# The stores of the results move from SyncE's turn to the end of ScalarE's turn

## The reference

```python
W = weights[condition]                       # 16 matrices of 128 x 128
x = x + einsum('bct,bcd->bdt', x, W)         # the "rows", one per batch entry

mask = (arange(L) < length[:, None])
u_m = x * mask[:, None, :]
K = 2.0 * einsum('hn,hnl->hl', Cs, exp(P)).real     # one kernel per channel, 2048 taps
y = irfft(rfft(u_m, 2*L) * rfft(K, 2*L), 2*L)[..., :L]
y = (y + u_m * D[:, None]) * mask[:, None, :]
x = x + y
```

## Time and profile before

| | us |
|---|---|
| median of 3 runs | 2345.85 (2344.41 to 2353.0) |
| the profiled execution's own time | 2358.94 |
| its span, first to last instruction | 2357.1 |

### The profile page before, as it was taken

The page is one execution under the profiler, slowest core; times in us unless marked ns, Lnnn a source line. Parts: engine busy times, 40 slices in busy tenths (PEclk is TensorE's granted clock), DMA queues, the critical chain, the costliest instruction groups (busy, mean ns, idle before and its releaser), DMA issues.

```text
span 2357.1 us, 61717 instructions
## 1 busy us (share of the span) xinstructions
PE 2174.2 (92%) x15101; PEld 1880.7 (80%) x15101; DVE 1699.5 (72%) x3359; ACT 1505.9 (64%) x4354; POOL 1175.0 (50%) x1862
## 2 busy tenths in 40 slices
PE   6777778999999999999999999899999999999999
PEld 2222226888888888888888888799999999999998
DVE  4999204777777777777777777677777777777776
ACT  4556556777777777777777777455555555555555
POOL 0994503666666666666666666333333333333331
PEclk9999999999999999999999999999999999999999
DMA  8999999999999999999999999889989999899887
GB/s 319 420 414 369 394 359 330 316 315 315 314 316 318 317 317 318 320 315 317 320 319 311 323 316 307 241 251 262 268 253 267 266 270 259 259 261 264 254 260 223
DMA packets 337444, 716.26 MB, mean 304 GB/s; under 512 B 39554, under 2 KB 170884, under 8 KB 337412
## 3 DMA queue, kind: packets, MB, share of 16 engines
q1 hardware_dynamic: 300548, 581.66, 79.7%
q10 hardware_dynamic: 36864, 134.23, 14.0%
HBM read 395.92 MB, written 319.82 MB: 304 GB/s over the span
## 4 chain that ended last, share of the span: by engine, by line
PE 36%; DMA 28%; DVE 9%; SPq 8%; issue 8%; ACT 6%; ACTq 4%; DVEq 0%; POOL 0%
DMA decay<-x_scratch 12%; DMA toep<-k_scratch 11%; PE bank L900 7%; PE bank L902 6%; PE bank L901 6%; DMA row_x<-in_x 5%; PE bank L882 4%; DVE decay L803 4%; PE bank L945 4%; PE bank L869 3%; PE bank L937 3%; SPq L339 3%; SPq L355 2%; DVE e_lo L786 2%; ACTq L521 2%
## 5 line engine op out<-in xcount | busy, mean ns | idle before, releaser
L791 DVE TENSOR_TENSOR u_lo<-bank,u_hi 128x512 fp32r<-128x512 f32 x512 | 352.2, 688 | 252.7 <-ACT u_hi L603 246.7
L797 DVE TENSOR_TENSOR s_lo<-state,s_hi 128x128 fp32r<-128x128 f32 x768 | 291.8, 380 | 236.7 <-ACT s_hi L615 235.4
L900 PE MATMUL bank<-t_hi,u_hi 128*128 128x256 f32 x1024 | 361.7, 353 | 43.1 <-DMA toep<-k_scratch 42.5
L612 ACT ACTIVATE state<-bank 128x128 f32<-128x128 f32 x768 | 213.9, 279 | 286.8 <-PE bank L902 149.5
L803 DVE COPY_PREDICATED decay<-mask,bank 128x512 f32<-128x512 uint8 x512 | 379.1, 741 | 23.8 <-PE bank L902 3.6
L945 PE MATMUL bank<-toep,u_odd 128*128 128x128 f32 x2048 | 392.8, 273 | 0.0
L546 ACT ACTIVATE row_y<-bank 128x512 f32<-128x512 f32 x512 | 301.4, 589 | 138.2 <-ACT row_y L546 38.7
L489 POOL TENSOR_TENSOR x_lo<-row_x,x_hi 128x256 fp32r<-128x256 f32 x496 | 371.5, 778 | 0.0
L869 PE MATMUL bank<-row_x,w_sel 128*128 128x512 f32 x528 | 265.5, 630 | 94.2 <-DMA row_x<-in_x 50.2
L466 POOL TENSOR_TENSOR outer<-par 128x256 f32<-128x256 f32 x512 | 321.5, 649 | 20.5
L463 POOL COPY par<-table 128x71 f32 (+1 forms) x256 | 62.4, 244 | 540.4 <-PE bank L902 540.4
(11 more groups left out here) (139 smaller groups left out, 5456.6 us busy)
## 6 DMA issues: line engine op xcount, KB each, us to landing
row_x<-in_x SPq DMA_DIRECT2D x256, 512.0 KB, 6.1
x_scratch<-row_y ACTq DMA_DIRECT2D x256, 512.0 KB, 5.6
decay<-x_scratch SPq DMA_DIRECT2D x256, 512.0 KB, 6.4
out<-decay SPq DMA_DIRECT2D x256, 512.0 KB, 4.4
b_scratch<-b_mat SPq DMA_DIRECT2D x128, 256.0 KB, 6.5
t_hi<-k_scratch SPq DMA_DIRECT2D x256, 128.0 KB, 4.7
t_lo<-k_scratch SPq DMA_DIRECT2D x256, 128.0 KB, 4.4
b_mat<-b_scratch SPq DMA_DIRECT2D x128, 256.0 KB, 5.0
```

The costliest lines, as they stand in the source:

```text
L791: v.tensor_tensor(u_lo[j % 2][:, blocks, :], t_bank[q][:, :].rearrange("s (k b) -> s k b", b=B), u_hi[j % 2][:, blocks, :].bitcast(fp32), ...
L900: mm(to, w_hi, m_hi, start=start, stop=False, skip_group_check=True)
```

## The change

`store_x2` is taken out of SyncE's turn and put, with the same wait and the same DMA, at the end of ScalarE's turn. Nothing else changes: TensorE's, VectorE's and GpSimd's instructions are the same.

```diff
@@ SyncE
-            def store_x2(seg, k, j):
-                sp.wait_ge(y_taken, k * NQ + NQ)
-                sp.dma_start(out[:, bass.ds(k - seg * H, 1), seg * SEG:(seg + 1) * SEG].rearrange("b a t -> b (a t)"), tile[j]).then_inc(x2_stored[j], 16)
@@ SyncE, channels()
                     if then and then[0] == 1:
                         load_edge(k + 2, j2)
-                    store_x2(seg, k, j)
@@ ScalarE
+            def store_x2(seg, k, j):
+                act.wait_ge(y_taken, k * NQ + NQ)
+                act.dma_start(out[:, bass.ds(k - seg * H, 1), seg * SEG:(seg + 1) * SEG].rearrange("b a t -> b (a t)"), tile[j]).then_inc(x2_stored[j], 16)
@@ ScalarE, channels()
                     if with_rows:
                         take_row(k + ROWS_FIRST, j, 1, row_bank)
                         store_row(k + ROWS_FIRST, j, 1, k + AHEAD)
+                    store_x2(seg, k, j)
```

## The result

Medians of four runs on one chip: 2438.46 us (2434.74 to 2441.51) against 2348.11 us before (2344.41 to 2353.0). The ratio is 1.0383, with a 95% interval of 1.0356 to 1.0409. I had forecast 2335, with a range up to 2368.

The account below looks back on a forecast made before the run. TensorE was taken as the bound, busy 386 of 400 us in segment 0 and 678 of 700 in segment 1. Segment 0's +4 and segment 1's -15 gave -11 us, from 2345.85 to 2335; 8-in-10 range 2304 to 2368.

Parts of the forecast that it names:

- ScalarE, segment 0: Loop `y_taken`, `keep_s` 1, states, last matmul closes through the store: 8.57 + 0.34 = 8.91 us, +4 us in all.
- my +0.34: Segment 0, us per channel by which `keep_s` 1 begins later after `y_taken`: +0.27 plus a quarter of the jump's 0.30.
- The loop through the end of the turn: ScalarE, segment 0: `keep_s` 1 waits for `y_taken` and the store's issue, beginning 0.70 us after `y_taken` instead of 0.43.
- SyncE, segment 0: x1's load goes out 1.40 us earlier, Toeplitz loads 0.57; Toeplitz stalls fall from 0.31 to some 0.05 us per channel.
- Segment 1: Whole segment: x1 stall nearly all goes, channel falls from 6.48 to 6.36 us, a gain of 15 us.
- the loop through `halve_edge` and VectorE: Segment 1: `y_taken`, `halve_edge`, VectorE's turn, `y_taken` takes 5.06 + 1.24 = 6.30 us and becomes the longest.
- The first, faster: Rival: ScalarE's wait is hidden, stalls won in full give 2284, half of it 2315 us; chance 0.20.
- The third, slower: Rival, segment 0: ScalarE's wait comes on top of late Toeplitz loads, +42 us less 15, 2373 us; chance 0.27.
- The second, full DMA engines: Rival: DMA engines set the pace, share 0.97 in segment 0, so no change, 2346 us; chance 0.13.
- the sign that I had named for it: Sign of the full-DMA-engines rival: the loads, issued earlier, land as much later.
- The sign that I named: Segment 0: L937's weight load waits for ScalarE's state in most channels, not in a third.

Follow-up runs that it names:

- run 2: Changed kernel without the register read of the row's index in `halve_w`, so all rows of segment 1 after the first four take matrix 0: 0.9910.
- run 5: Changed kernel with `halve_w`, register read included, moved in ScalarE's turn to just before the second half of the row's input: 0.9851.
- 10: Kernel before, with the row's store moved to SyncE as well, so ScalarE issues no DMA in the channels: 0.9996.
- run 12: Changed kernel, but SyncE waits for `y_taken` in segment 0 before it saves the edge, holding its loads back: 0.9899.
- run 4: Changed kernel with the store of the row's result in segment 0 moved from ScalarE to the end of SyncE's turn: 0.9911.
- run 14: Against the kernel before: in segment 0 SyncE stores channel k-1's result in turn k, behind the Toeplitz loads; in segment 1 ScalarE stores: 1.0735.
- run 9: On top of run 5, the kernel's store put before the row's load in SyncE's turn: 0.9825.
- run 7: Kernel before, with one more DMA of one 64-byte row on ScalarE behind the row's store in segment 0, without a wait: 1.0102.
- Run 3: Kernel before, with the wait for `y_taken` added at the end of ScalarE's turn, the store still on SyncE: 1.0028.
- run 1: Change applied in segment 1 alone: segment 0 stores from SyncE as in the kernel before, segment 1 from ScalarE: 0.9873.
- run 6: Kernel before, with `halve_w` and its register read moved to just before the second half of the row's input: 1.0103.

## Why the prediction was wrong

**ScalarE, segment 0: the step that failed.** I wrote that ScalarE's turn is "one unbroken run from `keep_s` 1 to the states of the next chunks", and took the loop as 8.57 us plus what the end of the turn adds. That the states stand on TensorE's path was right, and the loop did close through ScalarE (TensorE's weight load waits for them in 79 of 81 channels). But I took the run's own length as fixed, and it holds the 0.79 us of "issue" ahead of `w_sel`, which I had seen and didn't ask about. It became 1.86, because the register read in it went from 0.56 to 1.68 us: a term that I had put at nothing. With my +0.34 the loop would be 8.57 + 0.34 + 1.07 = 9.98 us; measured 9.88. Most of the rest is a small error in the +0.34 (below): with the measured +0.20 it is 9.84. Runs 2 and 5 take the read out of this path, and the loss is gone.

**What makes the read long: open.** The read runs in ScalarE's own list and has no wait in it, so in the kernel before only its spread (0.32 to 0.90 us) hints that it depends on something. The medians, 600 to 1400 us, by what the kernel does around it:

| run | x1's load issued, us after `y_taken` | stores on ScalarE | read, us |
|---|---|---|---|
| before | 0.72 | row | 0.56 |
| 10 | 0.76 | none | 0.56 |
| 12 | 0.74 | row and result | 0.84 |
| 4 | 0.08 | result | 0.82 |
| 14 | 3.34 | row | 0.99 |
| after | -0.67 | row and result | 1.68 |
| 5, read moved | -0.66 | row and result | 0.31 |
| 9, read moved | -0.65 | row and result | 0.73 |

Holding the loads back (run 12) or taking one store away (run 4) halves the read, so the 1.68 us needs both parts of the change. The stores with late loads add 0.28 us; early loads without the stores were tried by no run, since in run 14 x1's load went out late. ScalarE's own issues nearby aren't needed for a longer read either: runs 5 and 9 differ in SyncE's order alone. The mean load of the DMA engines isn't it: their share was 0.97 with a read of 0.56 us and 0.92 with one of 1.68. That the read and SyncE's issues lengthen each other would fit, but it is a guess that no run shows, and the 1.05 us of run 7 doesn't fit any of my theories.

**The loop through the end of the turn: right in kind, too large in size.** `keep_s` 1 begins 0.69 us after `y_taken` in the mean of segment 0 (predicted 0.70, with the jump 0.77), and at a jump 0.92 against 1.0. But before the change it began 0.49 us after it in the mean, not the 0.43 that I had read in one channel, so the step is +0.20 us and not +0.34. Run 3 (the wait) and run 5 (wait and store) show that by themselves they don't hurt: in run 5 both stand there, and TensorE doesn't wait for the state.

**SyncE, segment 0: the number came true by luck.** The Toeplitz stall fell to 0.07 us (predicted 0.05), and the loads did go out earlier: x1's by 1.39 us in the median (predicted 1.40), the first Toeplitz load by 1.50 (predicted 0.57, at most 1.40), since the kernel's store landed after 3.4 us instead of 4.4. But the slow pace helps here. Where the pace is restored, the stall is back: 36.9 us in the 89 channels of run 5, 0.41 each, 0.59 in run 2. There the kernel's store lands after 5.5 and 5.8 us, and SyncE stands waiting for it (193.5/87 = 2.2 us per wait in run 5), so the Toeplitz loads go out no earlier. Where they do, in run 9, they land no earlier. My 0.05 was true of a kernel that ran slowly enough.

**Segment 1: right in sign, short in size.** 6.28 us from channel 130 on; I had 6.36 from a loop of 6.30 through VectorE. It runs at TensorE's pace, 6.17 in most channels, with 6.5 at the jumps, where ScalarE's 0.53 us gap stands. The gain is 27 us; I had 15. VectorE idles still, (123.3 + 53.8)/112 = 1.58 us per channel, where I had said 0.3 or less. So the loop through `halve_edge` and VectorE that I had named does not close, and 6.36 was near 6.28 for another reason: the pace is TensorE's own work, as before, without the wait for x1.

**The rivals.** The first, faster, was right that the wait itself is hidden (runs 3 and 5), but segment 0's stalls were not won in any run. The third, slower, was right in sign only: it put the loss on the Toeplitz loads, which came in time, and at 42 us at most. Its mechanism, loads held by the kernel's store, appears once the read is out of the way (run 5). The second, full DMA engines, is refuted for this loss: the share fell to 0.92. For the stalls that are left it isn't: in run 9 the loads go out earlier and land as much later, the sign that I had named for it. Nor did the second issuing engine give segment 0 any bandwidth: 286 GB/s against 317.

**The sign that I named.** "The weight load of L937 waits for ScalarE's state in most channels" came true (79 of 81), for a reason that I had not foreseen.

## What to carry to other kernels

When work is moved to another engine, look at each "issue" gap in that engine's list and find the instruction that makes it: here it was a read into a register, whose median went from 0.56 to 1.68 us with what surrounded it, and the loop that closes through ScalarE paid the difference. Before blaming the new instruction, keep it and move its neighbour: here one moved line turned +3.8% into -1.5%. And a stage in which an edit gains can be kept alone, as in run 1, which gets nearly the same 1.3% without touching segment 0.

## What the hardware showed beside that

- The register read of one index took from 0.27 (run 6) to 1.93 us (run 14) in these runs. Some 5 us behind ScalarE's last DMA issue the median is 0.28 (run 6). Distance alone doesn't make it short, as run 9's 0.73 shows, 4.2 us behind it.
- After the store of a result, ScalarE's next operation begins 0.1 us behind the end of the issue in the median, and 0.44 us (segment 0) or 0.52 us (segment 1) where its loop jumps back. In the row stage it was 0.2 and 0.5 us, which I had taken for the price.
- SyncE's issue of `t_lo` has no wait ahead of it. Its median was 0.54 us before; in the changed kernel it is 1.31 us, in run 9 1.51 us (source view, ns):

```profile
L339 SPq DMA_DIRECT2D t_lo<-k_scratch x81: 553/1310/1730, 600.5 to 1392.9; - x81
```

In the changed kernel it overlaps with ScalarE's long read: by the medians the read runs from 1.01 to 2.69 us after `y_taken`, this issue from 2.06 to 3.29. In run 9 both are longer than in run 5 (the issue 1.51 against 0.68, the read 0.73 against 0.31) and don't overlap: the issue runs from 1.55 to 3.10, the read from 4.65 to 5.36.
